# A GRU on one Trainium2 core: ring of 22 steps instead of 14, two blocks of each turn fetched row by row from SP, one semaphore per chain and slot

## What is computed

```python
x = emb[item_seq]                       # 512 x 200 x 128, table of 12500 items
def step(h, x_t, m_t):                  # m_t: item != 0
    mx = x_t @ W + b_i                  # gates z, r, candidate: 3 x 128
    mh = h @ U + b_r
    z = sigmoid(mx[:, :D] + mh[:, :D])
    r = sigmoid(mx[:, D:2*D] + mh[:, D:2*D])
    hh = tanh(mx[:, 2*D:] + r * mh[:, 2*D:])
    return where(m_t, z * h + (1 - z) * hh, h)
probs = softmax(h_last @ Wout + bout)
```

## Time and profile before

| what | value |
| --- | --- |
| time, median of 3 runs | 1039.23 us (1037.85 to 1040.12) |
| the profiled execution | 1038.45 us |
| its span | 1036.5 us |
| granted TensorE clock | 0.995 of full speed |
| busy: PE, PE weight loads, DVE | 976.5, 760.8, 792.0 us |
| busy: ACT, POOL | 593.2, 765.7 us |
| table gathers of POOL (L359) | 734, mean 946 ns |
| row DMAs of SP (L275) | 1792 = 14 blocks of 128 |

### The profile page before, as it was taken

How to read it: one execution, slowest core, us unless ns; L and a number is a source line. 1 busy time by engine, 2 the same in 40 slices (tenths; PEclk the granted TensorE clock), 3 DMA queues, 4 the chain that set the end, 5 groups by cost and what they waited for, 6 DMA issues and landing times.

```text
span 1036.5 us, 20050 instructions
## 1 busy us (share of the span) xinstructions
PE 976.5 (94%) x5218; PEld 760.8 (73%) x5218; DVE 792.0 (76%) x2075; ACT 593.2 (57%) x1301; POOL 765.7 (74%) x807
## 2 busy tenths in 40 slices
PE   6999999999999999999999999998898888988986
PEld 4556888777777777777777777776666666766765
DVE  3444667888888888888888888887777877777776
ACT  2334555666666666666666666655555555555555
POOL 5677777777777777777777777777777777777773
PEclk9999999999999999999999999999999999999999
DMA  9997555555555555555555555555555555555553
GB/s 356 403 373 279 150 161 159 161 161 160 163 158 161 163 157 161 161 161 161 159 163 158 161 160 161 160 160 162 157 161 163 157 160 161 159 161 159 164 163 95
DMA packets 62053, 184.29 MB, mean 178 GB/s; under 512 B 16428, under 2 KB 19812, under 8 KB 62020
## 3 DMA queue, kind: packets, MB, share of 16 engines
q0 software_dynamic: 48640, 147.77, 49.6%
q1 hardware_dynamic: 11984, 35.24, 8.9%
q10 hardware_dynamic: 1396, 0.91, 0.3%
HBM read 157.78 MB, written 26.07 MB: 177 GB/s over the span
## 4 chain that ended last, share of the span: by engine, by line
PE 55%; POOL 27%; issue 10%; DMA 3%; DVE 3%; ACT 1%; DVEq 0%; SPq 0%; POOLq 0%; ACTq 0%
POOL arena L359 27%; PE bank L453 14%; PE bank L459 9%; PE bank L455 9%; PE bank L441 8%; PE bank L375 5%; PE bank L447 4%; DMA rows<-turned 2%; PE bank L422 1%; PE bank L427 1%; PE bank L423 1%; DVE h L630 1%; ACT cand L561 1%; DVE rh L625 1%; PE bank L380 1%
## 5 line engine op out<-in xcount | busy, mean ns | idle before, releaser
L359 POOL DMA_INDIRECT arena<-table,row_table x734 | 694.7, 946 | 223.9 <-issue 218.7
L559 ACT ACTIVATE bank<-bank,b_gates 128x256 f32<-128x256 f32 x400 | 179.2, 448 | 252.2 <-PE bank L459 252.2
L441 PE MATMUL bank<-ident,arena 128*128 128x128 f32 x1496 | 249.8, 277 | 40.4 <-DMA arena<-table,row_table 39.5
L453 PE MATMUL bank<-h,U_sb 128*128 128x256 f32 x800 | 265.9, 414 | 1.7 <-DVE h L630 1.6
L640 DVE SCALAR_TENSOR_TENSOR bank<-bank,cand 128x256 f32<-128x256 f32 x400 | 172.7, 432 | 121.7 <-ACT cand L561 118.9
L441 PEld LDWEIGHTS bank<-ident,arena 128*128 128x128 f32 x1496 | 184.5, 141 | 106.0 <-DMA arena<-table,row_table 67.8
L561 ACT ACTIVATE cand<-pre,bi 128x256 f32<-128x256 f32 x400 | 202.9, 507 | 86.4 <-DVE pre L634 86.4
L459 PE MATMUL bank<-h,U_sb 128*128 128x256 f32 x800 | 240.3, 382 | 0.0
L625 DVE SCALAR_TENSOR_TENSOR rh<-bank,br,r 128x256 f32<-128x256 f32 x400 | 193.5, 484 | 58.2 <-ACT r L557 55.2
L455 PE MATMUL bank<-h,U_sb 128*128 128x256 f32 x800 | 237.9, 379 | 0.0
L557 ACT ACTIVATE r<-bank,b_gates 128x256 f32<-128x256 f32 x400 | 189.8, 475 | 34.2 <-PE bank L453 30.7
(11 more groups left out here) (61 smaller groups left out, 249.9 us busy)
## 6 DMA issues: line engine op xcount, KB each, us to landing
arena<-table SPq DMA_DIRECT2D x1792, 1.5 KB
table<-proj SPq DMA_DIRECT2D x24, 768.0 KB, 5.3
arena<-table,row_table POOLq DMA_INDIRECT x734, 3.1
arena<-in_L_rec_emb SPq DMA_DIRECT2D x12, 512.0 KB, 10.4
rows<-turned SPq DMA_DIRECT2D x12, 512.0 KB, 10.3
raw<-rows,row_table POOLq DMA_INDIRECT x52, 4.8
seq<-in_r_item_seq ACTq DMA_DIRECT2D x1, 400.0 KB, 10.5
table<-proj SPq DMA_DIRECT2D x2, 192.0 KB
```

The lines of the kernel that those rows point to most:

```text
L359: pool.indirect_dma_start(ring_rows(s, k), None, table, bass.IndirectOffsetOnAxis(row_table[:, t, k:k + 1], 0)).then_inc(s_slot[s][k], 16)
L441: pe.matmul(dst[:, i * P:(i + 1) * P], ring_row(s, k, g), ident[:, :], start=(i == 0), stop=False, is_transpose=True, skip_group_check=True)
L453: pe.matmul(reset_sum[c], U_sb[:, D:2 * D], h[c][:, :], start=False, stop=True, skip_group_check=True).then_inc(s_reset[c], 1)
L559: act.activation(update_sum[c], update_sum[c], ACT.Sigmoid, bias=b_gates[:, 0:1]).then_inc(s_z[c], 1)
```

## The change

The ring gets 22 slots instead of 14: 8 full turns and 11 steps left. Two blocks of each turn are fetched by SP, (slot 4, block 3) and (slot 15, block 3), each with its own semaphore; SP's loop body holds both, and the first blocks of both slots are fetched ahead of the loop without a wait for PE. To have room for the ring, the buffers `turned` and `proj` of the stores become views of the arena, in slots 14 to 21; the arena's first 12500 columns hold the embeddings in that phase, as before. The offsets of SP's rows take two multiplications, one transpose and two small DMAs instead of one of each. The gathers of a chain in a slot share one semaphore, and PE waits once, for all gathers of the chain, before its first transpose; POOL waits likewise once per chain for n < 13.

```diff
--- before.py
+++ after.py
@@ -17,9 +17,8 @@
 CHAINS = ((0, 1), (2, 3))
 WIDTH = 2 * P
 RAW = 13
-RING = 14
-SLOW_STEP = 4
-SLOW_BLOCK = 3
+RING = 22
+SLOW = ((4, 3), (15, 3))
...
@@ -84,9 +83,14 @@
 
         arena = sb("arena", [P, RING * BLOCKS * GATES])
         raw = sb("raw", [P, RAW * BLOCKS * D])
-        turned = [sb(f"turned{q}", [P, CHUNK, D]) for q in range(STAGES)]
         turned_last = sb("turned_last", [P, 3, D])
-        proj = [sb(f"proj{q}", [P, GROUP, GATES]) for q in range(AHEAD)]
+
+        TURNED = (RING - AHEAD) * BLOCKS * GATES - STAGES * CHUNK * D
+        assert GROUP <= BLOCKS and ITEMS <= TURNED
+        turned = [arena[:, TURNED + q * CHUNK * D:TURNED + (q + 1) * CHUNK * D].rearrange(
+            "p (j n) -> p j n", j=CHUNK) for q in range(STAGES)]
+        proj = [arena[:, (RING - AHEAD + q) * BLOCKS * GATES:][:, 0:GROUP * GATES].rearrange(
+            "p (j n) -> p j n", j=GROUP) for q in range(AHEAD)]
...
@@ -173,12 +177,12 @@
         s_store = [sem(f"table_stored{q}") for q in range(AHEAD)]
         s_padrow = sem("pad_rows_stored")
 
-        s_slot = [[sem(f"slot{s}_block{k}_gathered") for k in range(BLOCKS)] for s in range(RING)]
+        s_slot = [per_chain(f"slot{s}_gathered") for s in range(RING)]
         s_offsets = sem("slow_offsets_ready")
         s_slow_turned = sem("slow_offsets_turned")
         s_slow_copied = sem("slow_offsets_copied")
         s_slow_line = sem("slow_offsets_on_one_partition")
-        s_slow = sem("slow_rows_fetched")
+        s_slow = [sem(f"slow{b}_rows_fetched") for b in range(len(SLOW))]
...
@@ -212,6 +216,16 @@
         def table_stores(q):
             return len(range(q, GROUPS, AHEAD)) + (3 if q == GROUPS % AHEAD else 0)
 
+        def load_offsets(eng, b, turn, first, n):
+            return nc.values_load_multi_w_load_instructions(
+                slow_line[b:b + 1, bass.ds(turn * P + first, n)], engines=[eng.engine],
+                min_val=0, max_val=(ITEMS + P) * ROW_BYTES,
+                skip_runtime_bounds_check_because="row numbers are clamped where they are made")[1]
+
+        def fetch_row(eng, b, p, offset):
+            return eng.dma_start(ring_rows(*SLOW[b])[p:p + 1, :].bitcast(U8),
+                                 table_bytes[:, bass.ds(offset, ROW_BYTES)])
+
         def columns(i):
             return arena[:, i * P:min((i + 1) * P, ITEMS)]
...
@@ -251,33 +265,33 @@
 
 
             sp.wait_ge(s_slow_copied, 1)
-            sp.dma_start(slow_line[:, :], slow_turned[:, :]).then_inc(s_slow_line, 16)
+            for b in range(len(SLOW)):
+
+                sp.dma_start(slow_line[b:b + 1, 0:(TURNS + 1 - b) * P],
+                             slow_turned[b * (TURNS + 1):2 * TURNS + 1 if b else TURNS + 1, :]
+                             ).then_inc(s_slow_line, 16)
             for q in range(AHEAD):
                 sp.wait_ge(s_store[q], 16 * table_stores(q))
+            for q in range(STAGES):
+                sp.wait_ge(s_rows[q], 16 * len(range(q, CHUNKS, STAGES)))
             sp.wait_ge(s_padrow, 16 * 2)
-            sp.wait_ge(s_slow_line, 16)
-            slot = ring_rows(SLOW_STEP, SLOW_BLOCK).bitcast(U8)
-
-            def slow_block(turn):
+            sp.wait_ge(s_slow_line, 16 * len(SLOW))
+
+            def slow_block(b, turn):
                 for first in range(0, P, BATCH_ROWS):
-                    _, offset = nc.values_load_multi_w_load_instructions(
-                        slow_line[0:1, bass.ds(turn * P + first, BATCH_ROWS)], engines=[sp.engine],
-                        min_val=0, max_val=(ITEMS + P) * ROW_BYTES,
-                        skip_runtime_bounds_check_because="row numbers are clamped where they are made")
-                    if first == 0:
-
-                        if isinstance(turn, int):
-                            sp.wait_ge(s_slot[SLOW_STEP][SLOW_BLOCK], 16)
-                        else:
-                            sp.wait_ge(s_free[1], (turn - 1) * RING + SLOW_STEP + 1)
+                    offset = load_offsets(sp, b, turn, first, BATCH_ROWS)
+                    if first == 0 and (not isinstance(turn, int) or turn > 0):
+
+                        sp.wait_ge(s_free[1], (turn - 1) * RING + SLOW[b][0] + 1)
                     for i in range(BATCH_ROWS):
-                        p = first + i
-                        sp.dma_start(slot[p:p + 1, :], table_bytes[:, bass.ds(offset[i], ROW_BYTES)]
-                                     ).then_inc(s_slow, 16)
-
-            slow_block(0)
-            with sp.Fori(1, TURNS + 1) as turn:
-                slow_block(turn)
+                        fetch_row(sp, b, first + i, offset[i]).then_inc(s_slow[b], 16)
+
+            for b in range(len(SLOW)):
+                slow_block(b, 0)
+            with sp.Fori(1, TURNS) as turn:
+                for b in range(len(SLOW)):
+                    slow_block(b, turn)
+            slow_block(0, TURNS)
...
@@ -324,11 +338,14 @@
             pool.wait_ge(s_copy, 3)
             pool.tensor_tensor(row_f, row_f, over_f, ALU.add).then_inc(s_idx, 1)
             pool.wait_ge(s_idx, 7)
-            pool.tensor_scalar(slow_offsets[:, :], row_f[:, SLOW_BLOCK, RAW + SLOW_STEP:STEPS:RING],
-                               float(ROW_BYTES), None, ALU.mult).then_inc(s_offsets, 1)
+            for b, (s, k) in enumerate(SLOW):
+                turns = len(range(RAW + s, STEPS, RING))
+                pool.tensor_scalar(slow_offsets[:, b * (TURNS + 1):b * (TURNS + 1) + turns],
+                                   row_f[:, k, RAW + s:STEPS:RING], float(ROW_BYTES), None, ALU.mult
+                                   ).then_inc(s_offsets, 1)
...
@@ -340,7 +357,7 @@
                     pool.indirect_dma_start(
                         raw_row(t, k), None, rows,
                         bass.IndirectOffsetOnAxis(row_table[:, t, k:k + 1], 0)
-                    ).then_inc(s_slot[t][k], 16)
+                    ).then_inc(s_slot[t][k // 2], 16)
...
@@ -351,15 +368,15 @@
                     if n >= RING:
 
                         pool.wait_ge(s_free[c], n - RING + 1)
+                    if n < RAW:
+                        pool.wait_ge(s_slot[n][c], 32)
                     for k in CHAINS[c]:
-                        if (s, k) == (SLOW_STEP, SLOW_BLOCK):
+                        if (s, k) in SLOW:
                             continue
-                        if n < RAW:
-                            pool.wait_ge(s_slot[n][k], 16)
                         pool.indirect_dma_start(
                             ring_rows(s, k), None, table,
                             bass.IndirectOffsetOnAxis(row_table[:, t, k:k + 1], 0)
-                        ).then_inc(s_slot[s][k], 16)
+                        ).then_inc(s_slot[s][c], 16)
...
             def turn_rows(t, c):
 
+                pe.wait_ge(s_slot[t][c], 32)
                 for i, k in enumerate(CHAINS[c]):
-                    pe.wait_ge(s_slot[t][k], 16)
                     last = pe.matmul(x_sum[c][:, i * P:(i + 1) * P], raw_row(t, k), ident[:, :],
                                      start=(i == 0), stop=True, is_transpose=True, skip_group_check=True)
                 last.then_inc(s_x[c], 1)
@@ -432,12 +449,12 @@
 
             def transpose_rows(turn, s, c):
 
+                gathered = sum((s, k) not in SLOW for k in CHAINS[c])
+                pe.wait_ge(s_slot[s][c], (turn + 1) * (16 * gathered) + (32 if s < RAW else 0))
                 for i, k in enumerate(CHAINS[c]):
                     for n, (dst, g) in enumerate(((reset_sum[c], 1), (cand_x[c], 2))):
-                        if n == 0 and (s, k) == (SLOW_STEP, SLOW_BLOCK):
-                            pe.wait_ge(s_slow, (turn + 1) * (P * 16))
-                        elif n == 0:
-                            pe.wait_ge(s_slot[s][k], turn * 16 + (32 if s < RAW else 16))
+                        if n == 0 and (s, k) in SLOW:
+                            pe.wait_ge(s_slow[SLOW.index((s, k))], (turn + 1) * (P * 16))
                         pe.matmul(dst[:, i * P:(i + 1) * P], ring_row(s, k, g), ident[:, :],
                                   start=(i == 0), stop=False, is_transpose=True, skip_group_check=True)
```

More of the change, by code:

```diff
@@ L111, in gru @@
         row_table = sb("row_table", [P, STEPS, BLOCKS], I32)
[L112 to L114 removed]
+        slow_offsets = sb("slow_offsets", [P, 2 * TURNS + 1])
+        slow_turned = sb("slow_turned", [2 * TURNS + 1, P], I32)
+        slow_line = sb("slow_line", [len(SLOW), (TURNS + 1) * P], I32)
         copy_i = sb("copy_i", [P, 1], I32)
@@ L402, in _ @@
                 project(i)
-            slow_bank = bank[1][0:TURNS + 1, 0:P]
-            pe.wait_ge(s_offsets, 1)
+            slow_bank = bank[1][0:2 * TURNS + 1, 0:P]
+            pe.wait_ge(s_offsets, len(SLOW))
             pe.wait_ge(s_tdve, CHUNKS + 1)
```

9 lines of the change are left out of this document (3 added, 6 removed).

## The result

The change took 1034.07 us (median of 6 runs, 1033.83 to 1034.48), the kernel before 1040.44 us beside it (median of 6, 1037.85 to 1041.48). The ratio is 0.9943 with a 95% interval of 0.993 to 0.9956: faster by 0.6%, 4.6 to 7.3 us. Two later measurements, each with the kernel before beside it, gave 0.9938 [0.9924, 0.9951] and 0.9937 [0.9922, 0.9952]. The profiled execution took 1033.86 us at a span of 1032.0.

A forecast was written before the change was run, and what follows sets the result against it. POOL's gathers were taken to set the end, with PE 40 us of slack. The last step's -4.35 (fewer gathers and pair wait included) plus 0.1 for SP's fetches took 1039.23 to 1034.9 us; 8-in-10 range 1033.3 to 1037.2.

The forecast's parts named there:

- Part 1: POOL's gathers: 731 instead of 734, so the last gather starts 3.75 us earlier, at 1018.55.
- Part 2: PE's last step, four gathers instead of three: last reset gate at 1023.15 instead of 1027.50, 4.35 us earlier.
- Part 3: PE's one wait per pair of gathers: no delay adds up; bounds 0 to 0.3 us, 0.2 taken.
- Rival B: Gain given back by a worse pair wait or longer gather period: within 2.1 us of now, 1038; chance 0.10.
- POOL never waits for the ring: Reading of the waits before the change: POOL's only idle time is issue, at most 0.3 us each.
- what costs PE less than that in the first phase can't move the end: Claim that PE's early delays under its 40 us of slack don't count, as POOL's gathers set the end.
- the 4.35: Forecast gain in us at the last reset gate, from fewer POOL gathers and the different last step.
- Part 4: SP's row fetches: 49.97 us per block, two per turn 99.9; SP keeps ahead of need, cost 0.
- Rival A: SP becomes the bound: at 54 us per block (T) the time is 1057; chance 0.06.
- margin of 20 us at n = 114: SP's 11th block, there at 651.5 where PE needs it at 671.4: SP's smallest margin.
- Part 5: The rest: offsets 0, fewer loop boundaries of 0.23 us swallowed, SP's fetches beside POOL's gathers 0.1 us.
- PE's slack: PE without waits for gathers would start the last step at 985 us, not near 1024: 40 us.

The follow-up runs named there:

- the pair kernel: The kernel before, ring of 14, with only the signal changed to one semaphore per chain and slot and one wait for a pair: 1039.16 us, ratio 1.0004.

## Why the prediction was right, and where it was not

**The time.** 1034.9 was forecast, 1034.07 measured, within 1033.3 to 1037.2. Of the profiles the forecast was close: span 1032.2 against 1032.0. Of the difference in the medians it was not: -4.3 forecast, -6.4, -6.5 and -6.1 in three measurements, and none of their intervals reaches under 4.6 us. That the absolute time agreed is luck: the median of before that I started from, 1039.23, was below the 1040.44 of the six runs beside the change.

**Part 1, the count: right.** 731 gathers; 8 more of them move the last one by 10.0 us at equal periods, and 4 more cost 5.1.

**Part 2, the last step: right in the sum.** The last reset gate was at 1023.16 (1023.15 forecast), by luck, as two errors cancel: POOL's last gather came at 1019.56 instead of 1018.55, and the landing took 3.11 instead of 4.10. I took 4.10 from the one row that was unusual; in the ring of 14 two more profiles have it above the usual 3.1 (3.56 and 4.19), in the ring of 22 none. With 3.1 for the landing after, the forecast would have been a microsecond lower.

**Part 3, the pair wait: right.** 1.0004 [0.9995, 1.0013] for it alone in the ring of 14, and in the change PE's steps keep up with POOL to the end. Rival B falls with it.

**What failed: "POOL never waits for the ring", and with it "what costs PE less than that in the first phase can't move the end".** The row was true of that execution, and of the next one that was profiled, but not of the pair kernel's. I didn't compare the two times at the place where the ring is tightest: the 56th gather at 173.76, the end of PE's last reads of slot 0 at 173.12. That is at most 0.64 us of margin, 0.36 with the 0.28 that a release takes, where I wrote 40. The sum lacked a term for it. Its size is bounded rather than measured: 1.40 us in one execution of the pair kernel, 0 in both profiles of the kernel before, and together with the late landing 1.6 us on average by the ring of 15 and 2.6 by the ring of 22 with one block. What the change gained beyond the 4.35, 1.8 to 2.2 us, lies between. The heaps in the runs of the kernel before fit a stall that some executions have, but none of its longer runs was profiled, and POOL's period, by which profiles differ by up to 2 us, could make heaps too. So how the sum divides stays open.

**Part 4, SP: right in its effect, wrong in its price.** SP did not stall PE, but it was through at 974.98, not 948: each taken branch costs it 2.6 to 3.1 us instead of 0.4, and the blocks themselves are slower than reckoned, 50.9 us back to back with the loop written out. A pair takes 104 us. That is T = 52.0, the figure that Rival A got with a stall of 4.10 us; that it is the same is chance, and by its reckoning the end doesn't feel it. It didn't. The forecast's margin of 20 us at n = 114 is 23 if it is counted from the end of SP's issuing (671.4 - 648.4), and it was 22 (688.4 - 666.0). But two errors cancel again: SP was 17.6 us late, and PE, which DVE's stalls held back, 17.0. With DVE's loop written out PE is there at 672.0, as forecast, and 4.6 us are left. So the 0.06 for that rival was low: with a ring of 20 it is the whole result.

**Part 5, boundaries: wrong in size.** I wrote "fewer boundaries of 0.23 us". There are fewer, and DVE's stall of about 3 us makes a step at each take 7.3 to 9.2 us. The cover I named, PE's slack, holds at these places: with DVE's loop written out the time is the same. The term of 0.1 us for SP's fetches beside POOL's gathers can't be seen: the period was 1.2503 to 1.2530 in the profiles of the change, 1.2507 and 1.2515 in those of the kernel before.

**Code fetches.** By the trace DVE and SP stall behind taken branches, and the traffic of code rose from 0.17 to 0.79 MB. That agrees with the rule of the Trainium skill (Runtime: NRT & Kernel Launch, Instruction fetch mechanics) that a taken branch out of the window stalls. The room for 512 instructions that the same section of the Trainium skill gives for most engines doesn't agree with DVE's trace. From one of DVE's branches to the next the trace has 333 instructions in the change, which stalls, and 303 with the ring of 20, which stalls too; with 228 (ring of 15) and 213 (ring of 14) the next instruction comes within 0.3 us. I had applied the rule to SP alone, whose body has 532; DVE, with the shorter code, showed the longer stall, and PE and ACT none. A fetch in straight code isn't without effect either, as the gathers beside it seem to be late.

## What to carry to other kernels

When one engine sets the end without a pause, count its instructions: each one is worth its period, and edits elsewhere are worth nothing until they run into a shared edge. Look for that edge where a buffer is first reused, and compare the two times there, not the sums of waits: a margin of 0.4 us in one profile can be a wait in another execution. A margin that comes out as forecast should be taken apart as well, since it may be two errors of one size. And when an engine is made to carry more because it has time left, reckon its work back to back, with its loop's branch, and ask which size of the ring would break it.

## What the runs showed that I had not expected

- A taken branch to a long loop body cost DVE about 3 us (2.9 to 3.4 in the change's first profile) and SP 2.6 to 3.1 us with bodies of 22 steps and of two blocks, and 0.3 and 0.4 us with 14 steps and one block. ACT goes on after 0.2 us in both, and PE shows no stall of its own there.
- POOL's period for the same gather differs from execution to execution: 1.2501 to 1.2530 us over the profiles, 2 us in 731 gathers. Its raw gathers differ with it, 1.2480 to 1.2511 us. Its cause is open.
- No gather took over 3.86 us to land without a fetch of code in its flight, and 22 with one took 3.9 to 4.9, where 3.1 is usual. Whether the fetch is the cause no edit has tested.
